# Cross-attention with an image-prompt branch on one core: own buffers for the split queries, and elementwise SBUF work moved from VectorE to GpSimd

## The reference

```python
q = heads(x @ W_q); k_t = heads(text @ W_k); v_t = heads(text @ W_v)
probs_t = softmax(q @ k_t.T * Dh**-0.5)
text_out = probs_t @ v_t
qsem = l2norm(probs_t @ text)                      # 512 wide, per head
fused = q @ (ip @ W_k_ip).T * Dh**-0.5 + 0.5 * qsem @ l2norm(ip).T
probs_ip = softmax(fused) * spatial_mask
out = (text_out + probs_ip @ (ip @ W_v_ip)) @ W_out + b_out + x
```

## Time and profile before

| quantity | value |
|---|---|
| median of 3 runs | 498.07 us (496.77 to 501.51) |
| the profiled execution, its own time | 496.4 us |
| its span, from the first to the last instruction | 494.2 us |
| mean granted TensorE clock | 0.931 of full speed |
| busy: PE, DVE, ACT, POOL | 428.0, 275.8, 202.2, 157.5 us |

### The profile page before, as it was taken

One profiled execution on the slowest core, in us unless ns is written; L12 is line 12 of the kernel. 1 busy time (PEld: TensorE's weight loads), 2 busy tenths in 40 slices (PEclk: granted clock), 3 DMA queues, 4 the chain that ended last, 5 costly groups with the idle time before them and its releaser, 6 DMA issues.

```text
span 494.2 us, 9417 instructions
## 1 busy us (share of the span) xinstructions
PE 428.0 (87%) x3620; PEld 340.8 (69%) x3620; DVE 275.8 (56%) x576; ACT 202.2 (41%) x479; POOL 157.5 (32%) x129
## 2 busy tenths in 40 slices
PE   3998799799878898998889898989798999799755
PEld 1377687677767786777678677867687868677633
DVE  0844544557166653675376827683667546734871
ACT  1403200635444426443454435634445255347510
POOL 2102240034313530181117311542135314423640
PEclk9998955979989889998999999999899999999996
DMA  7597893003830427030711272036202340000000
GB/s 241 98 227 203 148 227 64 22 0 101 153 51 2 125 48 140 1 121 16 149 28 64 61 130 61 21 102 123 67 2 60 70 86 1 2 11 25 1 12 12
DMA packets 33325, 38.00 MB, mean 77 GB/s; under 512 B 18457, under 2 KB 30713, under 8 KB 32505
## 3 DMA queue, kind: packets, MB, share of 16 engines
q1 hardware_dynamic: 33282, 37.42, 33.0%
HBM read 28.50 MB, written 8.81 MB: 75 GB/s over the span
## 4 chain that ended last, share of the span: by engine, by line
PE 44%; DMA 19%; DVE 16%; SPq 7%; issue 5%; ACT 4%; POOL 3%; POOLq 0%; ACTq 0%; DVEq 0%
PE PR L747 21%; PE Y L747 16%; DMA kst<-kd 15%; DVE pb L676 4%; DVE mx L653 3%; PE O L747 3%; SPq L393 3%; PE P L747 3%; DMA qd<-pb 2%; DMA et<-ctxT 2%; POOL pb L468 1%; POOL nrm L473 1%; DVE z L714 1%; SPq L316 1%; ACT big L545 1%
## 5 line engine op out<-in xcount | busy, mean ns | idle before, releaser
L468 POOL TENSOR_TENSOR pb<-pb 128x448 f32<-128x448 f32 x80 | 92.3, 1154 | 264.9 <-DVE pb L676 258.8
L747 PE MATMUL Y<-er,Gh 128*128 128x448 f32 x240 | 100.0, 417 | 14.1 <-DVE pb L676 10.4
L653 DVE TENSOR_REDUCE mx<-PR 112x1 f32<-112x371 f32 x160 | 80.0, 537 | 31.6 <-PE PR L747 29.3
L676 DVE TENSOR_TENSOR pb<-big,Y 128x448 f32<-128x448 f32 x120 | 72.5, 619 | 41.3 <-PE Y L747 40.1
L545 ACT ACTIVATE big<-P 128x448 f32<-128x448 f32 x120 | 64.6, 539 | 66.7 <-PE P L747 66.7
L747 PE MATMUL Y<-er,Gl 128*128 128x448 f32 x240 | 91.9, 383 | 0.0
L549 ACT ACTIVATE er<-big 128x448 fp32r<-128x448 f32 x120 | 69.3, 578 | 3.8
L747 PE MATMUL PR<-kst,qst 96*112 96x371 bf16 x160 | 54.0, 368 | 17.7 <-DMA kst<-kd 12.7
L747 PEld LDWEIGHTS Y<-er,Gh 128*128 128x128 f32 x240 | 48.5, 202 | 30.2 <-DVE pb L676 21.9
L747 PEld LDWEIGHTS Y<-er,Gl 128*128 128x128 f32 x240 | 48.8, 203 | 2.8
L747 PE MATMUL P<-qst,kst 99*128 99x112 bf16 x480 | 43.8, 216 | 1.7 <-ACT big L545 1.7
(11 more groups left out here) (124 smaller groups left out, 696.1 us busy)
## 6 DMA issues: line engine op xcount, KB each, us to landing
et<-ctxT SPq DMA_DIRECT2D x8, 752.0 KB, 4.5
kst<-kd SPq DMA_DIRECT2D x8, 720.0 KB, 7.4
kd<-ks SPq DMA_DIRECT2D x16, 288.0 KB, 2.9
kst<-kd SPq DMA_DIRECT2D x8, 480.0 KB, 9.5
qst<-qd SPq DMA_DIRECT2D x48, 70.0 KB, 2.4
kst<-kd SPq DMA_DIRECT2D x8, 240.0 KB, 10.6
qd<-ks SPq DMA_DIRECT2D x4, 336.0 KB, 5.6
vx<-xr SPq DMA_DIRECT2D x8, 140.0 KB, 2.2
```

Source lines behind the costliest of these rows:

```text
L468: pool.tensor_tensor(total, total, (pz, pm)[j], ALU.add).then_inc(s_S, 1)
L653: dve.tensor_reduce(mx[b % 2][:, h:h + 1], bank[0:S, 0:T], AX.X, ALU.max).then_inc(s_free[seq[u] % NR], 1)
L676: dve.tensor_tensor((pz, pm, pa[g % 2])[j], eb[g % 3][:, 448 * j:448 * j + 448], Y[y % 2][:, 0:448], ALU.mult).then_inc(s_P, 1)
L747: return pe.matmul(o, st, mv, start=start, stop=stop, **kw)
```

## The change

The split queries get five buffers of their own in the (still unused) tile `kst[1]`, which grows to 128 partitions, and a scratch tile there; the waits `q_written` of ACT, POOL and DVE for the keys go, and SP loads the constant rows of `kst[1]` later, ahead of its `load_k(1)`. The ip columns of the context come packed from the host, as one DMA (`ctxip`) in place of four. The elementwise work whose operands lie in SBUF moves from DVE to POOL: `El` for items from 2 on, the masking of `vr`, the residual plus bias, and of the ip chain the denominator's square, `tn`, three score operations, the subtraction, the mask and the product. What DVE keeps of the chain are the clamp, reciprocals, and the two reductions. The power is now -0.5, with EPS squared in the clamp, and the factor 0.5 lies in `nip`; the instruction with EPS (L712) and its reciprocal (L713) are gone, the denominator's square is new. `master_schedule()` is not changed.

```diff
-        qs = [ksf[:, 1344 * i:1344 * i + 1344].rearrange("p (j n) -> p j n", j=3) for i in range(2)] + [pb[:, 960:960 + 672].bitcast(bf16)...]
+        spare = kst[1][:, :, :].rearrange("p h t -> p (h t)").bitcast(f32)
+        qs = [spare[:, 672 * i:672 * i + 672].bitcast(bf16).rearrange("p (j n) -> p j n", j=3) for i in range(5)]
+        qr = spare[:, 3360:3808]
...
 # SP
-            ip = [(ET_IP[:, c, :]..., ctxT[:, :, c, IP0:NP].rearrange("b p n -> p b n")) for c in range(4)]
+            ip = [(ET_IP[:, :, :], ctxip), (hq[:, :, :], hm_q), (wkip_s, ...), (wvip_s, ...)]
...
-                    sp.wait_ge(s_spl, 6 + b + 1)
+                    sp.wait_ge(s_ksp, b + 1)
...
+                    if b == 1:
+                        q_written(sp)
+                    if b in (1, 2):
+                        sp.dma_start(kst[b][96:99, :, :], krow...).then_inc(s_kr[b], 16)
                     load_k(b)
 # ACT, POOL and DVE, first keys and first product
-                        q_written(act)
-                        q_written(pool)
-                        q_written(dve, 3)
 # DVE, split of q
-                    if i >= 3:
-                        dve.wait_ge(s_qw[i % 3], 16)
+                    if i == 5:
+                        q_written(dve, 1)
 # POOL, new
+                if u[0] == "El" and u[1] >= 2:
+                    pool.wait_ge(s_eh, 2 * b + u[2] + 1)
+                    filled(pool, ("V", b - 2, 2))
+                    pool.tensor_tensor(el[b % 2][:, sl, :], et[:, sl, :], eh[b % 2][:, sl, :].bitcast(f32), ALU.subtract).then_inc(s_el, 1)
+                if u[0] == "T" and i == 0:
+                    pool.tensor_tensor(vr[b % 2], vr[b % 2], hv[:, :], ALU.mult).then_inc(s_vb, 1)
                 if u[0] == "pw":
+                    pool.tensor_tensor(t1[:, hs], R[:, hs, 20], R[:, hs, 20], ALU.mult).then_inc(s_sd, 1)
                     pool.wait_ge(s_clamp, b + i + 1)
-                    pool.tensor_tensor(nrm[:, hs], ssq[:, hs], half[:, hs], ALU.pow).then_inc(s_pw, 1)
+                    link(pool.tensor_tensor(t1[:, hs], ssq[:, hs], halfm[:, hs], ALU.pow))
+                # r, part 0
+                        pool.wait_ge(s_rd, b + i + 1)
+                        pool.tensor_tensor(tn[:, hs, :], R[:, hs, 0:D], rden..., ALU.mult).then_inc(s_tn, 1)
+                # r, part 1
+                        link(pool.tensor_tensor(zz, R[:, hs, 16:20], t1..., ALU.mult))
+                        link(pool.tensor_tensor(zz, zz, nip..., ALU.mult))
+                        pool.tensor_tensor(zz, zz, Sip..., ALU.add).then_inc(s_zs, 1)
+                # r, part 2
+                        pool.wait_ge(s_zx, b + i + 1)
+                        pool.tensor_tensor(zz, zz, zb, ALU.subtract).then_inc(s_z, 1)
+                # p
+                        pool.wait_ge(s_zr, b + i + 1)
+                        link(pool.tensor_scalar(zm[:, hs], zm[:, hs], mask_s[:, 0:1], 0.0, ALU.mult, ALU.add))
+                        pool.tensor_tensor(pp, pp, zb, ALU.mult).then_inc(s_p, 1)
+                if u[0] == "cT":
+                    pool.tensor_tensor(res[b % 2][:, :], xs[b % 2], bias[:, :], ALU.add).then_inc(s_xb, 1)
 # DVE, what is left of the chain
+                elif k == "pw":
+                    dve.wait_ge(s_sd, b + i + 1)
+                    dve.scalar_tensor_tensor(ssq[:, hs], t1[:, hs], EPS * EPS, R[:, hs, 21], ALU.mult, ALU.max).then_inc(s_clamp, 1)
+                # r, part 0 (part 1: nothing)
+                        dve.reciprocal(rden[:, hs], R[:, hs, 20]).then_inc(s_rd, 1)
+                # r, part 2
+                        dve.wait_ge(s_zs, b + i + 1)
+                        dve.tensor_reduce(zx, z[:, hs, :], AX.X, ALU.max).then_inc(s_zx, 1)
+                # p
+                        dve.wait_ge(s_ze, b + i + 1)
+                        link(dve.tensor_reduce(zx, pe_[:, hs, :], AX.X, ALU.add))
+                        dve.reciprocal(zx, zx).then_inc(s_zr, 1)
 # PE
                 elif k == "cT":
+                    pe.wait_ge(s_tn, b + (2 if b == B - 1 else 1))
```

More of the change, by code:

```diff
@@ L149, in build @@
         qst = [sb(f"qst{i}", [99, H, S], bf16) for i in range(3)]
-        kst = [sb(f"kst{i}", [(99, 99, 128)[i], H, TP], bf16) for i in range(3)]
+        kst = [sb(f"kst{i}", [(99, 128, 128)[i], H, TP], bf16) for i in range(3)]
         et = sb("et", [128, 4, NP])
@@ L238, in build @@
         s_spl = sem("s_spl")
-        s_qw = [sem(f"s_qw{n}") for n in range(3)]
+        s_ksp = sem("s_ksp")
+        s_qw = [sem(f"s_qw{n}") for n in range(2)]
         s_kw = sem("s_kw")
@@ L264, in build @@
         s_R = sem("s_R")
+        s_sd = sem("s_sd")
         s_clamp = sem("s_clamp")
-        s_pw = sem("s_pw")
+        s_rd = sem("s_rd")
+        s_tn = sem("s_tn")
+        s_nip = sem("s_nip")
+        s_zs = sem("s_zs")
+        s_zx = sem("s_zx")
         s_z = sem("s_z")
         s_ze = sem("s_ze")
+        s_zr = sem("s_zr")
+        s_pl = sem("s_pl")
         s_p = sem("s_p")
@@ L295, in written, with q_written @@
             return 64 * b
-        def q_written(eng, slots=2):
-            for n in range(slots):
-                eng.wait_ge(s_qw[n], 16 * 2)
+        def q_written(eng, halves=2):
+            for n in range(halves):
+                eng.wait_ge(s_qw[n], 16 * 3)
         @block.sync
@@ L333, in _ @@
             sp.dma_start(wv_s, wv.rearrange("(c p) n -> p c n", p=128)).then_inc(s_wr_, 16)
[L334 to L338, removed]
+            ip = [(ET_IP[:, :, :], ctxip), (hq[:, :, :], hm_q), (wkip_s, wkip.rearrange("(c p) n -> p c n", p=128)),
+                  (wvip_s, wvip.rearrange("(c p) n -> p c n", p=128))]
+            rest = [(kst[i][96:99, :, :], krow.rearrange("r (h t) -> r h t", h=H)) for i in range(1)]
             rest += [(ident[:, :], ident_d), (hv[:, :], hm_v), (mask_s[:, :], mask), (bias[:, :], bout.partition_broadcast(S))]
@@ L386, in _ @@
                 if u == ("q", 2, 1):
-                    q_written(sp, 3)
+                    q_written(sp)
                     load_q(0)
@@ L431, in _ @@
             fill(half[:, :], 0.5)
+            fill(halfm[:, :], -0.5)
             pool.wait_ge(s_wl, 2)
@@ L438, in _, with link @@
             assert fills[0] == FILLS
+            chain = [0]
+            def link(ins):
+                chain[0] += 1
+                ins.then_inc(s_pl, 1)
+                pool.wait_ge(s_pl, chain[0])
             for u in order:
@@ L475, in _ @@
+                if u[0] == "cT":
+                    b = u[1]
+                    pool.wait_ge(s_xr[b % 2], 16 * (b // 2 + 1))
+                    if b == 1:
+                        pool.wait_ge(s_vw, 16)
+                    if b >= 2:
+                        pool.wait_ge(s_out[b % 2], 16 * (b // 2))
+                    pool.tensor_tensor(res[b % 2][:, :], xs[b % 2], bias[:, :], ALU.add).then_inc(s_xb, 1)
         @block.scalar
@@ L627, in _ @@
                     dve.wait_ge(s_kh, 3 * b + c + 1)
-                    if c == 0:
-                        dve.wait_ge(s_spl, 6 + b)
+                    if c == 0 and b:
+                        dve.wait_ge(s_ksp, b)
                     dve.tensor_tensor(kr[:, TP * c:TP * c + w], bank[:, 0:w], ks[:, 0, TP * c:TP * c + w],
@@ L694, in _ @@
                     hs = heads(b, i)
-                    w = hs.stop - hs.start
-                    zz, pp, zx = z[:, hs, :], pe_[:, hs, :], zm[:, hs]
-                    zb = zx.unsqueeze(2).broadcast_to([S, w, NIP])
+                    zx = zm[:, hs]
                     if k == "p":
                         dve.wait_ge(s_ze, b + i + 1)
-                        link(dve.tensor_reduce(zx, pp, AX.X, ALU.add))
-                        link(dve.reciprocal(zx, zx))
-                        link(dve.tensor_scalar(zx, zx, mask_s[:, 0:1], None, ALU.mult))
-                        dve.tensor_tensor(pp, pp, zb, ALU.mult).then_inc(s_p, 1)
+                        link(dve.tensor_reduce(zx, pe_[:, hs, :], AX.X, ALU.add))
+                        dve.reciprocal(zx, zx).then_inc(s_zr, 1)
```

123 lines of the change are left out of this document (64 added, 59 removed).

## The result

The changed kernel takes 490.7 us (median of four, 489.29 to 491.89), the kernel before 497.69 in the same comparison (496.77 to 501.51): a ratio of 0.9838, with a 95% interval of 0.9803 to 0.9872. I had forecast 501.5 and a range from 491 to 512: the sign is wrong.

| stretch | before, us | after, us | change | forecast |
|---|---|---|---|---|
| start, to the first row maximum | 62.08 | 59.29 | -2.8 | -2.5 |
| first maximum to `mT` of item 0 | 20.36 | 20.36 | 0 | 0 |
| item 0: to `mT` of item 1 | 37.19 | 36.10 | -1.1 | 0 |
| items 1 to 5: to `mT` of item 6 | 266.04 | 259.27 | -6.8 | +1.2 |
| item 6: to the last `mT` | 45.12 | 45.22 | +0.1 | +0.5 |

The account below looks back on a forecast made before the run. PE, busy 87%, was taken as the bound, with 17.8 us of waits for DVE to relieve. Terms -2.5 + 0 + 1.2 + 0.5 + 5 = +4.2 on 496.4 gave 500.6; forecast 501.5 us, range 491 to 512.

Parts of the forecast that it names:

- The start: Up to the first row maximum: one packed `ET_IP` load shortens SP's chain, -2.5 us, bounds 0 and -3.4.
- Item 0: Context split on POOL: DVE free sooner and POOL later cancel, 0 us, bounds -1 and +2.
- Items 1 to 5: Middle items: the moves to POOL cost +1.2 us over five items, bounds -4 to +6.
- Net +0.25 an item: Each of items 1 to 5: balance of -0.7 (split), +0.7 (later subtraction) and -0.5 (`p`), a small loss.
- The split's -0.7: Group 0 of items 1 to 5: PE's 0.66 us wait for DVE's product, behind a split, goes.
- The chain from the end of the additions to the end of the subtraction: Group 1 onward of items 1 to 5: ip chain as one POOL line, to grow by 1.4 us.
- the forecast's own low end: Items 1 to 5: with every operation cost at its low end, an item gains 0.75 us.
- The rule of the Trainium skill: All moved operations: GpSimd takes about twice VectorE's time, 0.48 us for 80 elements; total 505 us.
- the forecast's first part: Every item: whatever comes after `mT` ends against the load of the keys, so only time before `mT` counts.
- Item 6: No split or keys: subtraction behind two POOL additions +1.0, `p` -0.5; +0.5 us, between 0 and +1.4.
- The last item: Chain in halves: POOL becomes the line to the last product for `pT`, +5 us, bounds 0 to +9.5.
- The faster one: Rival, whole kernel: POOL's line is short, low-end costs, -6.5 us, 491.5 on the median; chance 0.22.

Follow-up runs that it names:

- e11_pack: The kernel before with only the packed `ET_IP` load in place of four (`hq` and `wkip` loads swapped); 496.65 us, one execution.
- e8_best: `e6_tail67` with `El` of item 2 on VectorE as well; 484.3 us, ratio 0.9782.
- e7_dose: The changed kernel with `tn` of items 0 to 5 done twice on GpSimd, 0.73 us more per stage; 497.07 us, ratio 0.9977.
- e3_el_dve: The changed kernel with `El` of items 2 to 7 back on VectorE; 494.5 us, ratio 0.9868.
- e1_start: The kernel before with the new start alone, all elementwise work where it was; 497.52 us, ratio 0.9961.
- r_after: The changed kernel run again, unchanged, for a second trace; 491.12 us.
- e12_stall: The changed kernel with four unused products on VectorE ahead of the 18th maximum in items 0 to 5; 510.73 us, ratio 1.0284.
- e9_fill_e1: `e1_start` with seven extra TensorE products in its wait for a maximum, items 2 to 7; 496.1 us, ratio 1.0002.
- e10_fill_e8: `e8_best` with nine extra TensorE products in its wait for a product just before `mT`, items 2 to 7; 493.58 us.
- e4_last_dve: The changed kernel with the last item's ip chain back on VectorE, its powers still on GpSimd; 490.6 us, ratio 0.9811.
- e6_tail67: The changed kernel with the ip chain of items 6 and 7 back on VectorE, their powers still on GpSimd; 487.99 us, ratio 0.983.
- b2_before: The kernel before run again, unchanged, for a second trace; 499.99 us, one execution.

## Why the prediction was wrong

**The start: right.** SP in the changed kernel, to hold against the earlier trace rows; the forecast had the load of queries near 40.8 and the first maximum near 59.6 (PE's row below, to hold against the earlier trace rows):

```profile
19.89 0.76 SPq L358 DMA_DIRECT2D ET_IP<-ctxip  x1
...
40.22 2.64 SPq L317 DMA_DIRECT2D qst<-qd  x6
```

```profile
59.29 0.53 PE L788 MATMUL PR<-kst,qst 96*112 96x371 bf16 x1 [5.36 <-DMA kst<-kd]
```

The forecast gave the waits for q's slots nothing and the packing all; by `e11_pack` the slots may be up to 2.8 us of the gain.

**Item 0: 0 forecast, -1.1 measured, a little past the bound.** `El` of item 2 does cost 1.2 there (`e8_best`), inside the bounds; but the mean granted clock of the stage was 0.83 before and 0.89 after, which I hadn't counted.

**Items 1 to 5: the step that failed, "Net +0.25 an item".** Its structure held: one line on GpSimd from the additions to the scores, two stops of DVE in it, the wait for maxima down to a third and that for products longer, and by `e7_dose` the line decides. Its sizes were too long. The split's -0.7 came out (-0.67 by `e3_el_dve`). The chain from the end of the additions to the end of the subtraction was to grow by 1.4 and grew by 0.3: 11.66 before, 11.96 after. The power took 3.55 instead of the 3.80 that I carried over from the earlier trace rows (0.25), `tn` 0.73 instead of 0.89 (0.16), the three scores 1.0 instead of 1.17, key split and subtraction 0.15 less together, the handovers some 0.4 instead of 0.7. With the 0.6 from `p` an item at full clock gains 1.03, 5.2 for five; the forecast's own low end was 0.75, since it had the power and the handovers in no bound. I took the middle between two bounds for each operation (0.39 for 80 elements; 0.33 in the trace), and nearly all lay on the same side of it.

The power's 0.25 is not its new exponent. In the kernel before, it took 3.80 in the six stages where VectorE's `tn` was running as it began, and 3.55 in the one where `tn` began 2.84 us later, with the same exponent (timeline):

```profile
457.48 3.55 POOL L473 TENSOR_TENSOR nrm<-ssq,half 112x20 f32<-112x20 f32 x1
```

The halves of the last item took 2.28 and 1.65 with either exponent. In every trace the longer time goes with a `tn` that runs as the power begins, so the move itself shortened the power, which the forecast had said doesn't shrink.

The rule of the Trainium skill (GPSIMD Engine Reference, section Performance versus the Vector engine), twice VectorE's time, would have made it 505 by the forecast's estimate. The trace disagrees for small operands: 0.33 on GpSimd against 0.24 on an undisturbed VectorE. And VectorE wasn't undisturbed; the first score there, in `e1_start` (lines by form, and the sixth of the seven in a timeline):

```profile
L711 DVE TENSOR_TENSOR z<-R,t 112x80 f32<-112x80 f32 x7 | 6.2, 883 | 0.2
422.15 0.24 DVE L711 TENSOR_TENSOR z<-R,t 112x80 f32<-112x80 f32 x1
```

Six of the seven ran beside GpSimd's additions and took 0.98 to 1.01 us (268.79 above is one); at 422.15 GpSimd stood, and it took 0.24. The same operation takes 330 ns on GpSimd. The rows of before had shown this: the subtraction of 0.24 in the earlier trace rows takes 0.84 in the earlier trace rows, where it runs beside an addition.

**The clock in the items: not in the forecast at all.** The rest of the -6.8 is -1.6. In the two traces the stretches up to `mT` got 10.3 us shorter, 5.2 of it at full clock and 5.1 by falls that before has there and the changed kernel has less of, and the stretches behind `mT` got 3.6 longer, as the forecast's first part says: what comes after `mT` ends against the keys. Before's items vary by some 8 us from trace to trace (348.4 and 349.0, 356.1 in `e1_start`), those of the kernels with both moves by 5 (338.6 for `e8_best` to 343.6 for `r_after`; without those with a filler, a dose or another order of loads). That the moves change where the clock falls is shown by the counts and, with a longer wait than the old one, by `e12_stall`. How many of the median's 7 us this is stays open: `e9_fill_e1` is almost without falls in its trace, its fastest execution, and its median didn't fall, and why `e10_fill_e8` brought them back behind another wait I can't say.

**Item 6: right (+0.1 for +0.5). The last item: right in sign and nearly in size** (+3.8 for +5): from the end of the additions to the last product for `pT` it is 25.22 us before and 28.95 after. The forecast put item 6's chain and both halves of the last on one line by their operations. By `e4_last_dve` and `e6_tail67`, 0.7 us belong to the halves and 2.5 to item 6's chain, and some 1.1 of these, as an estimate from `b2_before`, are a fall of the clock that the forecast didn't have. So a part of the nearness is luck.

**The rivals.** The faster one, "the line is short", is what happened: its 491.5 on the median against 490.7. It was given 0.22, and had -4 for the items and nothing for the tail, where -6.8 and +3.8 came. That its total was so near is luck: its two errors cancel.

## What to carry to other kernels

Before pricing an operation on another engine by size, look at what it costs where it is: beside GpSimd's additions a VectorE operation of 80 elements took 0.99 us, and the chain's move was a gain of 0.36 us an item, though VectorE alone takes 0.24 and GpSimd 0.33. Test such moves stage by stage: in the last two items here, the chain back on VectorE made the tail 3.2 us shorter. And ask of every wait of TensorE what follows it: here one of 1.6 us ahead of a dense stretch made the stage up to 2.5 us longer by the clock (37.53 in `e1_start`, against 35.05 without a fall in `b2_before`), and one ahead of a wait brought none that the wait didn't cover.

## What was not expected of the hardware

Two-way slowing between VectorE and GpSimd was larger than I allowed for: an 80-element operation of VectorE took 0.99 us beside GpSimd's additions and 0.24 alone, GpSimd's power 3.80 us beside the start of VectorE's `tn` and 3.55 without it; in `e12_stall` four VectorE products of 112x448 took 4.04 us, and GpSimd's 80-element score went from 0.33 to 0.71. The clock fell within 2.2 us after stops of TensorE of 1.6 us, in 15 of 20 stages and not in the other five.
